# First-layer product in three two-part products, inputs split a chunk early, native products side by side, stores first on the load engine

## The chip, the core and the metric

One core of a Trainium2 chip runs the whole kernel. It has TensorE (PE, with its weight loads shown apart as PEld), VectorE (DVE), ScalarE (ACT), GpSimd (POOL, which issues the indexed gathers) and SyncE (SP, which issues the plain loads and stores). The metric is device time of one execution in microseconds (us): median of three runs, 5016.33 us before the change.

## The reference

Two graph layers run over 12500 nodes and 200000 edges, which are sorted by their target `dst`. What matters here is the first one:

```python
wk = relu(e @ k_w1 + k_b1) @ k_w2 + k_b2        # e: [E, 64], weights per edge
wv = relu(e @ v_w1 + v_b1) @ v_w2 + v_b2
k  = wk * sum_s sh[:, s] * (x[src] @ Cqk[:, s, :])   # s = 0..8, 64 -> 128
v  = wv * sum_s sh[:, s] * (x[src] @ Cv[:, s, :])
attn = einsum('ehd,ehd->eh', q[dst], k)         # softmax over the edges of a node
upd  = segment_sum(v * softmax(attn), dst)
x    = layernorm(x + batchnorm(x @ W_self + upd @ W_out))
```

The second layer takes the mean of the edges' features per node (a segment sum of `e`), and passes it with `x` through three small dense layers. Everything is float32. (In the code the roles of source and target in the index are those of the prepared inputs.)

## The kernel before

A first block prepares tables and weights. The main block, on which nearly all of the time is spent, goes over the edges in 392 chunks of 512. After it come a short block that mends segments over tile borders, and the node work.

**Two-part numbers.** A native float32 product on TensorE is slow, so the large products are made of parts: a float32 value is rounded to the type `float32r` (names that end in `hi`), the rest is what is left (`lo`), and a product is taken as hi*hi + lo*hi + hi*lo, three fast products. The tensor products (L825, L827, L828) and the second dense layer (L837 to L840) are done so. Native float32 are: the turns of the gathered rows and of the edge features (transposes, L797 and L813), the first dense layer (L807), and the segment sums (L855).

**One chunk, in short names.** PE: X turns the gathered rows `gx` (L797). H is the first dense layer into `hbank` (L807; `w1` against `e2`, a tile that holds two chunks, one in each half of the partitions). TP is 56 products (`tensor_products`). F turns the features of both chunks of a pair back into `hbank` (L813, only where `c.r` is odd). S0 and S1 are the halves of the segment sums (`sums`, L855): each has two products of a 0/1 matrix `seg` with the rows `rv`. EW is 16 products (`edge_weights`, L837 to L840). A and its sister turn scores and maxima, each once in four chunks (L879, L883). ACT copies out of PSUM (`ww` L572, `hid` L586, `rv` of F L595, `ot` L609), rounds to the high part (`zhi` L580, `hidhi` L601) and makes `seg` in `segments`: four ACTIVATE into `far` (L625), then one into `seg` (L630). DVE makes `z`, all of the low parts, the scores and the scans. POOL issues four gathers `gx` (L530) and four gathers `gq` (L535) for a chunk, and each fourth chunk one of another kind and a small copy.

**What sets the order.** Each engine has a function `step(t, ...)` written out by hand; `steps` calls it for every t (with a hardware loop of UN = 8 steps in the middle), and an engine runs its instructions in that order, each behind its semaphore waits. In step t the front works on chunk c = t+1, TP on chunk t, and the segment sums on b = t-6 (`LAG`). `segments(b+1)` on ACT makes the matrix that PE uses in the next step, in `sums(b, 0)` behind that step's TP. SP's order is loads of the harmonics `shb`, of the features, of the row `drow` for `segments`, of the masks `nmf` and `nmb` (the same numbers, one element apart), and then the store of the rows.

The few lines that the prediction's steps touch, on ACT and on PE:

```python
if c.r % 2 == 1:
    feature_rows(c + (-1))      # ACT, waits for F (et_full)
...
if (b + 1).there():
    segments(b + 1)             # ACT, sets seg_done
...
if half == 0:                   # PE, sums(b, 0)
    pe.wait_ge(pv_done, n)
    pe.wait_ge(seg_done, n)
```

Of the kernel before, what the change touches and what calls it, by code (L numbers as in the profile page):

```python
# [84 lines left out]
def steps(engine, step):  # L85
# [12 lines left out]
assert FINDS * TURNS + (NC + LAG + 1 - R0 - UN * TURNS) >= NT + 1 >= FINDS * TURNS  # L98


def gnn_kernel(nc, xg, xT, idx, dnow, dbefore, dlast, shT, eT, Wq, Ctp, W1, b1, Wk2, Wv2, b2, Wout, Wself, gamma_beta,
# [3 lines left out]
    newd = dram("newd", (EP + P,), bf16)  # L105
# [5 lines left out]
    with ctx:  # L111
# [7 lines left out]
        chi = sb("chi", [P, ST, KV], f32r)  # L119
        clo = sb("clo", [P, ST, KV], f32r)  # L120
        w1 = sb("w1", [P, 2, P])
        b1c = sb("b1c", [P, 1])
        w2hi = sb("w2hi", [P, KV], f32r)
        w2lo = sb("w2lo", [P, KV], f32r)
        b2hl = sb("b2hl", [P, KV], f32r)
        ones = sb("ones", [P, P], f32r)
# [12 lines left out]
        idx_all = sb("idx_all", [P, 2 * EC], i32)  # L139
        ndcol = sb("ndcol", [P, EC])  # L140
# [11 lines left out]

        load = sem("load")
# [3 lines left out]
        with ExitStack() as prep:  # L157
# [3 lines left out]
            ctp = ps("ctp", [P, ST, KV])  # L161
            w2 = ps("w2", [P, KV])
# [10 lines left out]
            npad = ps("npad", [2, P // 2], bf16)  # L173
# [24 lines left out]
            with nc.Block() as block:  # L198
                @block.sync
                def _(sp):  # L200
# [20 lines left out]
                    sp.wait_ge(neg_made, 3)  # L221
                    sp.dma_start(newd[0:EP].rearrange("(p c) -> p c", p=P), neg[:, :]).then_inc(tables_stored, 16)
                    sp.dma_start(newd[EP:EP + P].rearrange("(p c) -> p c", p=2), npad[:, :]).then_inc(tables_stored, 16)
# [6 lines left out]
                    sp.wait_ge(tables_stored, 64)  # L230
# [62 lines left out]
                def _(dve):  # L293
# [13 lines left out]
                    v.memset(npad[:, :], -BIG).then_inc(neg_made, 1)  # L307
# [11 lines left out]
                    dve.wait_ge(neg_made, 2)  # L319
# [16 lines left out]
                    dve.wait_ge(w_split, 6)  # L336
# [34 lines left out]
        with ExitStack() as main:  # L371
# [7 lines left out]
            nmf = ms("nmf", [P, 2, P], bf16)  # L379
            nmb = ms("nmb", [P, 2, P], bf16)  # L380
# [40 lines left out]
            et_full, et_done = sem("et_full"), sem("et_done")  # L421
            at_full, mf_done, mr_done, mt_full, mg_done, below_done = (
# [12 lines left out]
            with nc.Block() as block:  # L435
                @block.sync
                def _(sp):
# [27 lines left out]
                    def masks(g):  # L465
# [4 lines left out]
                        for ahead, tile in ((0, nmf), (1, nmb)):  # L470
# [86 lines left out]
                def _(act):  # L557
# [74 lines left out]
                    def step(t, find, fetch, count):  # L632
# [17 lines left out]
                        if b.there():  # L650
                            sums(b, 1)
# [804 lines left out]
```

## Time and profile before

| | |
|---|---|
| median of 3 runs | 5016.33 us (5014.75 to 5017.49) |
| the profiled execution | 5049.76 us, span 5047.8 us |
| mean granted TensorE clock | 0.975 |
| PE busy | 4772.7 us (95%) |
| DVE busy | 4058.6 us (80%) |
| POOL busy | 3713.3 us (74%), and 0.3 us before each gather that is not counted as busy |
| ACT busy | 3414.7 us (68%) |
| moved by DMA | 1006.45 MB, mean 199 GB/s |

A busy share is a mean over the whole span. The 0.975 comes from the end of the kernel: in the long main part the granted clock is 1.00. A matmul's record is longer than the time that it holds the engine, since matmuls are pipelined: what one costs is read from the distance between the starts of records. A native float32 matmul leaves two records.

### The profile page before, as it was taken

What the parts mean: (1) busy time and instruction counts of PE and PEld (TensorE: products, weight loads), DVE (VectorE), ACT (ScalarE), POOL (GpSimd) and SP (SyncE); (2) the same over time, 40 slices, a digit from 0 to 9 for tenths busy, and PEclk for the clock granted to TensorE, in tenths of its full rate; (3) what the DMA queues carried; (4) which work ended last, traced back from release to release, by engine and by line L of the source; (5) the groups of instructions that cost most, each with busy time, mean ns of one, the idle gap of its engine ahead of it and who ended that gap; (6) DMA issues with size and microseconds to landing.
All of it is one profiled execution on the core that took longest, in us unless ns stands there. A gap on an engine that the chain in (4) does not pass through costs nothing. (4 is left out here: it accounts for less than half of the span.)

```text
span 5047.8 us, 115383 instructions
## 1 busy us (share of the span) xinstructions
PE 4772.7 (95%) x35582; PEld 4503.5 (89%) x35582; DVE 4058.6 (80%) x5044; ACT 3414.7 (68%) x6495; POOL 3713.3 (74%) x3494
## 2 busy tenths in 40 slices
PE   7999999999999999999999999999999999998256
PEld 6999999999999999999999999999999999998143
DVE  5888888888888888888888888888888888886435
ACT  2677677677777767767777677777777777776137
POOL 3777777777777777777777777777777777774460
PEclk9999999999999999999999999999999999998578
DMA  8899999999999999999999999999999999996220
GB/s 218 202 215 210 208 210 214 208 214 210 212 207 214 213 208 213 211 210 211 211 213 211 207 216 213 216 214 214 213 216 212 214 214 216 212 213 158 91 68 26
DMA packets 693458, 1006.45 MB, mean 199 GB/s; under 512 B 120054, under 2 KB 378168, under 8 KB 693160
## 3 DMA queue, kind: packets, MB, share of 16 engines
q1 hardware_dynamic: 574856, 753.93, 65.7%
q0 software_dynamic: 112960, 242.16, 22.7%
q10 hardware_dynamic: 5600, 9.83, 0.7%
q8 instruction: 22, 0.36, 0.0%
q14 instruction: 20, 0.16, 0.0%
HBM read 826.64 MB, written 178.93 MB: 199 GB/s over the span
## 5 line engine op out<-in xcount | busy, mean ns | idle before, releaser
L825 PE MATMUL psum<-chi,zhi 128*128 128x256 f32 x7840 | 2316.9, 301 | 2.2 <-DVE rv L731 2.1
L535 POOL DMA_INDIRECT gq<-qtab,idxs x1568 | 1881.1, 1200 | 478.0 <-issue 475.8
L828 PE MATMUL psum<-clo,zhi 128*128 128x256 f32 x7840 | 2144.4, 282 | 0.0
L530 POOL DMA_INDIRECT gx<-in_xg,idxs x1568 | 1555.4, 992 | 465.0 <-issue 453.5
L827 PE MATMUL psum<-chi,zlo 128*128 128x256 f32 x6272 | 1768.4, 282 | 0.0
L825 PEld LDWEIGHTS psum<-chi,zhi 128*128 128x128 f32 x7840 | 1478.6, 189 | 99.3 <-issue 99.3
L828 PEld LDWEIGHTS psum<-clo,zhi 128*128 128x128 f32 x7840 | 1476.2, 188 | 0.0
L827 PEld LDWEIGHTS psum<-chi,zlo 128*128 128x128 f32 x6272 | 1183.6, 189 | 93.0 <-issue 93.0
L685 DVE TENSOR_TENSOR z<-psum,shb 128x1536 f32<-128x1536 f32 (+1 forms) x784 | 1130.5, 1483 | 126.2 <-PE psum L797 118.7
L580 ACT ACTIVATE zhi<-z 128x1536 fp32r<-128x1536 f32 (+1 forms) x784 | 993.5, 1267 | 247.9 <-DVE z L685 244.0
L710 DVE TENSOR_TENSOR zlo<-z,zhi 128x1536 fp32r<-128x1536 f32 (+1 forms) x784 | 922.2, 1217 | 0.0
L609 ACT ACTIVATE ot<-psum 128x400 f32<-128x400 f32 x784 | 389.0, 496 | 518.0 <-PE psum L855 513.2
L706 DVE TENSOR_TENSOR hidlo<-hid,hidhi 128x512 fp32r<-128x512 f32 x392 | 271.5, 693 | 536.3 <-ACT hidhi L601 526.2
L855 PE MATMUL psum<-rv,seg 128*128 128x200 f32 x3136 | 669.9, 337 | 20.8 <-DVE rv L693 16.7
L855 PEld LDWEIGHTS psum<-rv,seg 128*128 128x128 f32 x3136 | 512.3, 192 | 27.3 <-DVE rv L693 19.6
L625 ACT ACTIVATE far<-drow,ndcol 128x128 f32<-128x128 bf16 x1568 | 501.5, 390 | 13.1 <-issue 0.5
L837 PE MATMUL psum<-b2hl,ones 128*128 128x256 f32 x1568 | 496.8, 317 | 4.8 <-DVE hidlo L706 4.8
L840 PE MATMUL psum<-w2lo,hidhi 128*128 128x256 f32 x1568 | 442.4, 282 | 0.0
L839 PE MATMUL psum<-w2hi,hidlo 128*128 128x256 f32 x1568 | 441.8, 282 | 0.0
L838 PE MATMUL psum<-w2hi,hidhi 128*128 128x256 f32 x1568 | 441.4, 282 | 0.0
L595 ACT ACTIVATE rv<-psum 128x512 f32<-128x512 f32 x196 | 117.3, 598 | 465.1 <-PE psum L813 465.1
L572 ACT ACTIVATE ww<-psum 128x1024 f32<-128x1024 f32 x392 | 397.1, 1013 | 15.7 <-PE psum L840 15.6
(210 smaller groups left out, 6335.1 us busy)
## 6 DMA issues: line engine op xcount, KB each, us to landing
shb<-in_shT SPq DMA_DIRECT2D x392, 640.0 KB
shb<-in_shT SPq DMA_DIRECT2D x392, 512.0 KB
rows<-ot SPq DMA_DIRECT2D x392, 416.0 KB
e<-in_eT SPq DMA_DIRECT2D x392, 128.0 KB
drow<-rankd SPq DMA_DIRECT2D x392, 128.0 KB
gx<-in_xg,idxs POOLq DMA_INDIRECT x1568
gq<-qtab,idxs POOLq DMA_INDIRECT x1568
qtab<-qs ACTq DMA_DIRECT2D x25, 256.0 KB, 5.7
```

Of the source, the lines that this page charges most:

```text
L530: nc.gpsimd.indirect_dma_start(out=gx[:, s, k, :], out_offset=None, in_=xg[:, :], in_offset=bass.IndirectOffsetOnAxis(ap=ids[:, k:k + 1], ...
L535: nc.gpsimd.indirect_dma_start(out=gq[:, s, k, :], out_offset=None, in_=qtab[:, :], in_offset=bass.IndirectOffsetOnAxis(ap=ids[:, TC + k:T ...
L580: f(zhi[:, s, j, :], z[:, j, :], ACT.Copy).then_inc(zhi_done, 1)
L625: f(far[:, k * P:(k + 1) * P], drow[:, s, k * P:(k + 1) * P], ACT.Abs, bias=ndcol[:, bass.ds(b.value() * TC + k, 1)]).then_inc(far_done, 1)
L685: v.tensor_tensor(z[:, j, :], xbank.unsqueeze(1).broadcast_to([P, n, CH]), shb[:, s, j, :], ALU.mult).then_inc(z_done, 1)
L710: rest = lambda j: v.tensor_tensor(zlo[:, s, j, :], z[:, j, :], zhi[:, s, j, :].bitcast(fp32), ALU.subtract).then_inc(zlo_done, 1)
L825: mm(tpb[:, k, :], zhi[:, s, j, e], chi[:, j, :], start=(j == 0), stop=False)
L827: mm(tpb[:, k, :], zlo[:, s, j, e], chi[:, j, :], start=False, stop=False)
L828: last = mm(tpb[:, k, :], zhi[:, s, j, e], clo[:, j, :], start=False, stop=(j == ST - 1))
L837: mm(wb[:, k, :], ones[:, :], b2hl[:, :], start=True, stop=False)
L840: last = mm(wb[:, k, :], hidhi[:, e], w2lo[:, :], start=False, stop=True)
L855: last = mm(gbank[:, 256 * k:256 * k + O + D + H], seg[:, s, t * P:(t + 1) * P], rv[:, b.slot(UN), t, :], start=True, stop=True)
```

## The change

It does these things:

1. The first dense layer is taken in three two-part products. `w1` is split once, in the first block, into `w1hi` and `w1lo`. The features of a pair of chunks are split as well: ACT makes `e2hi` (`features_first_part`) and DVE `e2lo` (`features_rest`), once for two chunks, in the step before the pair's first product.
2. The segment sums are of chunk a = t-7 rather than b = t-6, and they stand on PE around X and H: S0, X, H, S1, TP, F, EW. The natives thus lie side by side (but for H, which is native no more). `seg_done` is waited for as before.
3. ACT's step has a new order. It starts with the copy of S0, takes `hidden` before `zhi`, `hidhi` before the second part of `zhi`, and ends with `segments(b)`, which stands behind `feature_rows`.
4. SP's step starts with the store (of chunk t-8), and loads `drow` for t-5 rather than t-4.
5. The masks are loaded once into `nmf`, one element wider, and the backward scan reads it shifted.
6. Some SBUF is freed earlier (`edges.close()`), and in the last block several semaphores become one for each engine.

```diff
@@ steps @@
-    for n in range(R0 + UN * TURNS, NC + LAG + 2):
+    for n in range(R0 + UN * TURNS, NC + LAG + 3):
...
@@ first block, DVE @@
+                    v.tensor_copy(w1hi[:, :, :], w1[:, :, :]).then_inc(w_split, 1)
...
+                    v.tensor_tensor(w1lo[:, :, :], w1[:, :, :], w1hi[:, :, :].bitcast(fp32), ALU.subtract)
...
@@ main block, SP @@
-                            sp.wait_ge(h_full, c.value() - 2)
+                            sp.wait_ge(e2lo_done, c.turn(2) - 1)
...
-                        for ahead, tile in ((0, nmf), (1, nmb)):
-                            src = newd[bass.ds(g.value() * CH + ahead, GT * P)].rearrange("(t e) -> t e", t=GT)
-                            sp.dma_start(tile[:, s, :], src.unsqueeze(1).broadcast_to([GT, H, P])).then_inc(nm_in[s], 16)
+                        src = newd[bass.ds(g.value() * CH, GT * P)].rearrange("(t e) -> t e", t=GT)
+                        sp.dma_start(nmf[:, s, 0:P], src.unsqueeze(1).broadcast_to([GT, H, P])).then_inc(nm_in[s], 16)
...
                     def step(t, find, fetch, count):
+                        if (t + (-LAG - 2)).there():
+                            store(t + (-LAG - 2))
                         if (t + 2).there():
                             harmonics(t + 2)
                         if (t.r + 3) % 2 == 0 and (t + 3).there():
                             features(t + 3)
-                        if (t + (2 - LAG)).there():
-                            targets(t + (2 - LAG))
+                        if (t + (1 - LAG)).there():
+                            targets(t + (1 - LAG))
...
-                        if (t + (-LAG - 1)).there():
-                            store(t + (-LAG - 1))
@@ main block, ACT @@
+                    def features_first_part(c):
+
+                        act.wait_ge(e_in[c.r // 2 % 2], 32 * (c.turn(4) + 1))
+                        if c.old(2):
+                            act.wait_ge(h_full, c.value())
+                        f(e2hi[:, :], e2[:, c.r // 2 % 2, :], ACT.Copy).then_inc(e2hi_done, 1)
...
-                        c, b = t + 1, t + (-LAG)
+                        c, b, a = t + 1, t + (-LAG), t + (-LAG - 1)
+                        if a.there():
+                            sums(a, 0)
+                        if t.there():
+                            edge_weights(t)
                         if b.there():
                             weights(b)
-                        if t.there():
-                            edge_weights(t)
+                        if c.there():
+                            hidden(c)
+                        if a.there():
+                            sums(a, 1)
+                            maxima(a)
+                        if (c + 1).there() and c.r % 2 == 1:
+                            features_first_part(c + 1)
                         if c.there():
                             z_first_part(c, 0)
-                            hidden(c)
+                            hidden_first_part(c)
                             z_first_part(c, 1)
-                            hidden_first_part(c)
                             if c.r % 2 == 1:
                                 feature_rows(c + (-1))
                         if b.there():
-                            sums(b, 0)
-                            maxima(b)
-                        if (b + 1).there():
-                            segments(b + 1)
-                        if b.there():
-                            sums(b, 1)
+                            segments(b)
@@ main block, DVE @@
+                    def features_rest(c):
+                        dve.wait_ge(e2hi_done, c.turn(2) + 1)
+                        if c.old(2):
+                            dve.wait_ge(h_full, c.value())
+                        v.tensor_tensor(e2lo[:, :], e2[:, c.r // 2 % 2, :], e2hi[:, :].bitcast(fp32), ALU.subtract).then_inc(e2lo_done, 1)
...
                             hidden_rest(c)
+                        if (c + 1).there() and c.r % 2 == 1:
+                            features_rest(c + 1)
+                        if c.there():
                             z_rest(c)
@@ main block, PE @@
                     def hidden(c):
-                        s = c.r // 2 % 2
-                        pe.wait_ge(e_in[s], 32 * (c.turn(4) + 1))
+                        pe.wait_ge(e2lo_done, c.turn(2) + 1)
...
-                        mm(hbank, w1[:, c.r % 2, :], e2[:, s, :], start=True, stop=True).then_inc(h_full, 1)
+                        k = c.r % 2
+                        mm(hbank, w1hi[:, k, :], e2hi[:, :], start=True, stop=False)
+                        mm(hbank, w1hi[:, k, :], e2lo[:, :], start=False, stop=False)
+                        mm(hbank, w1lo[:, k, :], e2hi[:, :], start=False, stop=True).then_inc(h_full, 1)
...
                     def step(t, find, fetch, count):
-                        c, b = t + 1, t + (-LAG)
+                        c, a = t + 1, t + (-LAG - 1)
+                        if a.there():
+                            sums(a, 0)
                         if c.there():
                             turned_x(c)
                             hidden(c)
+                        if a.there():
+                            sums(a, 1)
                         if t.there():
                             tensor_products(t)
                         if c.there() and c.r % 2 == 1:
                             turned_features(c + (-1))
-                        if b.there():
-                            sums(b, 0)
                         if c.there():
                             edge_weights(c)
-                        if b.there():
-                            sums(b, 1)
```

The line numbers shift: L595 (`rv` of F) becomes L611, L609 (`ot`) L625, L615 L631, L625 (`far`) L641, L630 (`seg`) L646, L661 (`signs`) L680, L572 (`ww`) L581; on PE L797 becomes L829, L813 L847, L837 to L840 L871 to L874, L855 L889, L879 L913.

On ACT, in a step with F, this is what stands behind the turned features before the change (from the first ACTIVATE that waits for F to the copy of the second half of the sums):

```order
329 L591 REGISTER_ALU
330 L593 REGISTER_ALU [waits et_full]
331 L595 ACTIVATE rv<-psum 128x8x64 [waits sum_full]
332 L605 REGISTER_ALU
333 L609 ACTIVATE ot<-psum 128x2x200 [waits rows_stored0,sum_full]
334 L615 ACTIVATE ot<-mg 128x4x8 [waits ota_done]
335 L625 ISA [waits drow_in1,seg_done]
...
344 L629 ISA [waits far_done]
345 L630 ACTIVATE seg<-far 128x512 [waits sum_full]
346 L605 REGISTER_ALU
347 L609 ACTIVATE ot<-psum 128x2x200 [waits sum_full]
```

And after it, from the second part of `zhi` to the copy that begins the next step:

```order
338 L589 ACTIVATE zhi<-z 128x1024 [waits tp_full,z_done]
339 L607 REGISTER_ALU
340 L609 REGISTER_ALU [waits et_full]
341 L611 ACTIVATE rv<-psum 128x8x64 [waits sum_full]
342 L636 ISA
343 L641 ISA [waits drow_in0,seg_done]
...
352 L645 ISA [waits far_done]
353 L646 ACTIVATE seg<-far 128x512 [waits sum_full]
354 L621 REGISTER_ALU
355 L625 ACTIVATE ot<-psum 128x2x200 [waits rows_stored0,sum_full]
356 L581 ACTIVATE ww<-psum 128x1024 [waits vv_done,w_full]
```

The copies of the sums have moved away from between; the `seg` made here is now the one of the sums at the head of PE's next step.

On PE, before the change, from the end of a TP with F to the second dense layer:

```order
1064 L828 MATMUL psum<-clo,zhi 128x256
1065 L811 REGISTER_ALU
1066 L813 MATMUL psum<-idn,e 128x128 [waits hid_done]
1067 L813 MATMUL psum<-idn,e 128x128 x3
1068 L846 REGISTER_ALU
1069 L848 REGISTER_ALU [waits seg_done,pv_done]
1070 L855 MATMUL psum<-rv,seg 128x200 [waits otb_done,et_done]
1071 L855 MATMUL psum<-rv,seg 128x200
1072 L837 MATMUL psum<-b2hl,ones 128x256 [waits ww_done,hidlo_done]
```

And after it, from the last product of the second dense layer over the border to the next step:

```order
1112 L874 MATMUL psum<-w2lo,hidhi 128x256
1113 L912 REGISTER_ALU [waits attn_done]
1114 L913 MATMUL psum<-idn,attn 128x128 [waits mg_done]
1115 L880 REGISTER_ALU
1116 L882 REGISTER_ALU [waits seg_done,pv_done]
1117 L889 MATMUL psum<-rv,seg 128x200 [waits otb_done,et_done]
1118 L889 MATMUL psum<-rv,seg 128x200
1119 L827 REGISTER_ALU [waits x_gathered2]
1120 L829 MATMUL psum<-idn,gx 128x128 [waits z_done]
1121 L829 MATMUL psum<-idn,gx 128x128 x3
...
1123 L839 MATMUL psum<-e2hi,w1hi 128x512 [waits et_done,hid_done,e2lo_done]
```

S0 stood behind TP and F, with X and H ahead; now it stands behind EW (and A), and X, H, S1 and TP are queued behind it.

## Rows read from the trace of the kernel before

**Rows 1.** Busy time by stretch: engines' busy us (instructions), granted clock, DMA share, GB/s.
```profile
400.00:2400.00 2000.00, 1978.51 (x15133) 1886.84 (x15132) 1691.59 (x2054) 1416.55 (x2692) 1576.05 (x1454) 1.00 0.95 211
3000.00:4600.00 1600.00, 1600.00 (x12279) 1529.58 (x12278) 1371.15 (x1665) 1148.27 (x2189) 1251.50 (x1181) 1.00 0.96 214
```

**Rows 2.** Who waited for whom, whole span: us in total, times, longest.
```profile
DVE hidlo L706 <- ACT hidhi L601: 526.2, 384, 2.5
ACT rv L595 <- PE psum L813: 465.1, 196, 2.9
PE psum L797 <- DMA gx<-in_xg,idxs: 43.5, 22, 16.0
```

**Rows 3.** PE's timeline, a chunk with F and A: start, us, line, xcount.
```profile
2513.89 0.60 PE L797 MATMUL psum<-idn,gx 128*128 128x128 f32 x4
2514.33 1.02 PE L807 MATMUL psum<-e,w 128*128 128x512 f32 x2
2514.79 0.68 PE L825 MATMUL psum<-chi,zhi 128*128 128x256 f32 x1
2515.31 0.28 PE L827 MATMUL psum<-chi,zlo 128*128 128x256 f32 x1
...
2521.78 0.28 PE L828 MATMUL psum<-clo,zhi 128*128 128x256 f32 x1
2521.90 0.60 PE L813 MATMUL psum<-idn,e 128*128 128x128 f32 x4
2522.34 0.84 PE L855 MATMUL psum<-rv,seg 128*128 128x200 f32 x4
...
2523.13 0.28 PE L838 MATMUL psum<-w2hi,hidhi 128*128 128x256 f32 x1
...
2524.92 0.84 PE L855 MATMUL psum<-rv,seg 128*128 128x200 f32 x4
2525.60 0.27 PE L879 MATMUL psum<-idn,attn 128*128 128x128 f32 x1
2525.70 0.60 PE L797 MATMUL psum<-idn,gx 128*128 128x128 f32 x4
```

**Rows 4.** ACT's timeline, the same chunk.
```profile
2519.64 0.63 ACT L601 ACTIVATE hidhi<-hid 128x512 fp32r<-128x512 f32 x1
2522.61 0.60 ACT L595 ACTIVATE rv<-psum 128x512 f32<-128x512 f32 x1 [2.35 <-PE psum L813]
2523.21 0.51 ACT L609 ACTIVATE ot<-psum 128x400 f32<-128x400 f32 x1
...
2523.95 1.28 ACT L625 ACTIVATE far<-drow,ndcol 128x128 f32<-128x128 bf16 x4
2525.36 0.63 ACT L630 ACTIVATE seg<-far 128x512 f32<-128x512 f32 x1
```

**Rows 5.** DVE's timeline, the same chunk.
```profile
2520.30 0.69 DVE L706 TENSOR_TENSOR hidlo<-hid,hidhi 128x512 fp32r<-128x512 f32 x1 [1.53 <-ACT hidhi L601]
2520.91 2.36 DVE L710 TENSOR_TENSOR zlo<-z,zhi 128x1536 fp32r<-128x1536 f32 x2
```

**Rows 6.** POOL's timeline, the same chunk.
```profile
2519.95 0.94 POOL L535 DMA_INDIRECT gq<-qtab,idxs  x1 [0.30 <-issue]
2521.19 2.29 POOL L535 DMA_INDIRECT gq<-qtab,idxs  x1 [0.30 <-issue]
```

**Rows 7.** All instructions that touch the tile gx: ns min/median/max, first and last start.
```profile
L797 PE MATMUL psum<-idn,gx x1568: 271/273/476, 78.1 to 4620.5; 128*128 128x128 f32 x196
```

**Rows 8.** PE's timeline at one of its waits for a gather.
```profile
958.20 0.84 PE L855 MATMUL psum<-rv,seg 128*128 128x200 f32 x4
961.32 0.65 PE L797 MATMUL psum<-idn,gx 128*128 128x128 f32 x4 [2.28 <-DMA gx<-in_xg,idxs]
```

**Rows 9.** Timeline of PE and PEld at 4631: a weight load, and its matmul.
```profile
4631.11 0.65 PEld L855 LDWEIGHTS psum<-rv,seg 128*128 128x128 f32 x4
4631.23 0.84 PE L855 MATMUL psum<-rv,seg 128*128 128x200 f32 x4
```

More of the change, by code:

```diff
@@ L151, in gnn_kernel, with eb @@
         banks = [psum[:, i * 512:(i + 1) * 512] for i in range(8)]
+        edges = ctx.enter_context(ExitStack())
+        def eb(name, shape, dt=fp32):
+            return edges.enter_context(nc.sbuf_tensor(name, shape, dt))
+        chi = eb("chi", [P, ST, KV], f32r)
+        clo = eb("clo", [P, ST, KV], f32r)
+        w1hi = eb("w1hi", [P, 2, P], f32r)
+        w1lo = eb("w1lo", [P, 2, P], f32r)
+        b1c = eb("b1c", [P, 1])
+        w2hi = eb("w2hi", [P, KV], f32r)
+        w2lo = eb("w2lo", [P, KV], f32r)
+        b2hl = eb("b2hl", [P, KV], f32r)
+        ones = eb("ones", [P, P], f32r)
+        idx_all = eb("idx_all", [P, 2 * EC], i32)
+        ndcol = eb("ndcol", [P, EC])
         load = sem("load")
@@ L161, in gnn_kernel @@
             ctp = ps("ctp", [P, ST, KV])
+            w1 = ps("w1", [P, 2, P])
             w2 = ps("w2", [P, KV])
@@ L378, in gnn_kernel @@
             drow = ms("drow", [P, 2, CH], bf16)
-            nmf = ms("nmf", [P, 2, P], bf16)
-            nmb = ms("nmb", [P, 2, P], bf16)
+            nmf = ms("nmf", [P, 2, P + 1], bf16)
+            e2hi = ms("e2hi", [P, CH], f32r)
+            e2lo = ms("e2lo", [P, CH], f32r)
             hid = ms("hid", [P, CH])
@@ L744, in segment_maxima @@
                         dve.wait_ge(at_full, n)
[L745 removed]
+                        dve.wait_ge(nm_in[s], 16 * (g.turn(2 * GC) + 1))
                         if g.old(GC):
                             dve.wait_ge(mt_full, n - 1)
[L748 removed]
+                        v.tensor_tensor_scan(mf[:, :], nmf[:, s, 0:P], sbank[:, 0:P], -BIG, ALU.add, ALU.max).then_inc(mf_done, 1)
                         dve.wait_ge(mf_done, n)
[L750 removed]
+                        v.tensor_tensor_scan(mr[:, ::-1], nmf[:, s, P:0:-1], mf[:, ::-1], -BIG, ALU.add, ALU.max).then_inc(mr_done, 1)
                     def below_maxima(g):
@@ L885, in _ @@
                     steps(pe, step)
+        edges.close()
         with ExitStack() as mend:
@@ L1085, in gnn_kernel @@
             st_d, st_a, st_pe = sem("stats_dve"), sem("stats_act"), sem("stats_pe")
-            SS = {k: sem(f"{k}_made") for k in ("r", "y", "dd", "sq", "lg", "rs", "x1", "s0", "h0", "h1", "y2", "dd2", "sq2",
-                                                "lg2", "rs2", "o")}
-            prod_made = sem("products_made")
-            PRODUCTS = ("mean", "var", "z0", "z1", "z2", "mean2", "var2")
+            MADE = {"pe": ("mean", "var", "z0", "z1", "z2", "mean2", "var2"),
+                    "act": ("r", "sq", "lg", "rs", "h0", "h1", "sq2", "lg2", "rs2"),
+                    "dve": ("y", "dd", "x1", "s0", "y2", "dd2", "o")}
+            made_by = {e: sem(f"blocks_made_by_{e}") for e in MADE}
             def wait_made(engine, name, i, j):
-                if name in PRODUCTS:
-                    engine.wait_ge(prod_made, (i * len(PRODUCTS) + PRODUCTS.index(name)) * GN + (j + 1))
-                else:
-                    engine.wait_ge(SS[name], i * GN + (j + 1))
+                for e, names in MADE.items():
+                    if name in names:
+                        engine.wait_ge(made_by[e], (i * len(names) + names.index(name)) * GN + (j + 1))
             with ExitStack() as fin1:
@@ L1293, in product @@
                                 wait_made(pe, after, i, j)
-                                t.matmul(bank_of(j), lhsT[:, :], W(src, j), start=True, stop=True).then_inc(prod_made, 1)
+                                t.matmul(bank_of(j), lhsT[:, :], W(src, j), start=True, stop=True).then_inc(made_by["pe"], 1)
                         def turn(i):
```

50 lines of the change are left out of this document (19 added, 31 removed).

## The prediction

> **What bounds the kernel now.** I read the busy times by stretch first, then the waits, then the timelines of PE, ACT, DVE and POOL over one chunk, and last the view of one tile, for the whole main loop. By stretch, PE is busy for all of 3000 to 4600 us and for 1978.51 of 2000 us before that, at a granted clock of 1.00 [rows 1]. So the order of PE's instructions and what each costs there sets the time; other engines count only where PE waits for them. The waits show one such place of weight: before X, for gathered rows, 43.5 us in 22 waits, of which one of 16.0 us is the start; 21 are left with 27.5 us [rows 2].
>
> What each piece costs is read from the distances of PE's starts [rows 3]. X: 2513.89 to 2514.33, 0.44 us. TP: from its second product at 2515.31 to its last at 2521.78 there are 54 steps, 0.1198 each, so 56 take 6.71. H is what is left of 2514.33 to 2521.90: 7.57 - 6.71 = 0.86. F: 0.44. S0 and EW: 2522.34 to 2524.92, 2.58; the 16 products of EW at nearly the step of TP's are 1.91, S0 is 0.67. S1: 0.68. A: 0.10. The sum is 11.81, which is the distance from X to X: nothing is idle. A chunk without F and A is 11.27. A pair of chunks has one F and on average one A or its sister: 2 x 11.27 + 0.44 + 0.10 = 23.08, 11.54 per chunk. Over the whole loop, the last chunk's X is at 4620.5 (less 0.3, as that is its fourth turn) and the first at 78.1 [rows 7]: 4542 us over 391 chunks, 11.617. The 0.08 above 11.54 is 31 us in all, which is the waits for gathers.
>
> **The change, part by part.**
>
> *H in three products.* 0.86 goes. No row shows a float32r product of 512 columns. The nearest is that of 256 columns at 0.1198. Twice that is 0.24, the upper end; 512 columns at 2.4 GHz, the level that a granted clock of 1.00 is, are 0.213, the lower end. I take 0.1198 plus 256 columns more at 2.4 GHz, 0.226. Three are 0.68 (0.64 to 0.72), the saving 0.18 per chunk (0.14 to 0.22), and over 392 chunks -71 us (-55 to -86).
> The Trainium skill (TensorE: Matmul & The Clock Gate, section "Wait — 56ns, not 53.3ns?") gives N / 2.4 GHz plus 2.5 ns from start to start. By that, as an estimate, three would take 0.65 and the saving be 83 us. At 256 columns it gives 0.109 where the rows have 0.1198, so the trace does not agree, and I stay with the rows.
>
> *Splitting the features.* ACT's `e2hi` and DVE's `e2lo` have the size of `hidhi` and `hidlo`, 0.63 and 0.69, once for a pair [rows 4, 5]. ACT's lies in the same step in which it waits 2.35 us for F; DVE waits 1.53 us for `hidhi` in each chunk, in total 526.2 us [rows 2, 5], and `hidhi` now comes earlier. Nothing for both. Without that cover `e2lo` would cost 0.69 per pair, 135 us.
>
> *The place of S0 and S1.* Moving them costs PE no time by itself: in rows 3 the change from float32r to native and back (TP to F to S0 to EW) shows no gap. What changes is when S0 comes, and what it waits for. It waits for `seg_done`. Before, `seg` was made on ACT in step t and used behind TP in step t+1, some 8 us later. Now `segments(b)` is the last thing in ACT's step t and S0 of the same chunk is the first in PE's step t+1. In a step with F, ACT stands in `feature_rows`, which waits for F (2.35 us in rows 4; 465.1 us in 196 waits, rows 2), and `segments` is queued behind it. So from the start of F on PE, called 0:
> - ACT starts `rv` (L595) at 0.71 (2521.90 to 2522.61) and its next ACTIVATE 0.60 later, at 1.31; now that is `far`.
> - From the start of `far` at 2523.95 to the end of `seg`, 2525.36 + 0.63 = 2525.99, are 2.04: `seg` is ready at 3.35 [rows 4].
> - A finished ACT operation lets the next engine start 0.03 later (`hidhi` ends at 2520.27, `hidlo` starts at 2520.30, rows 4 and 5); then `seg` is loaded as weights, 0.12 before the matmul [rows 9]. S0 can start at 3.50.
> - PE has F and EW to do until then: 0.44 + 1.91 = 2.35, with A 2.45.
> PE then stands idle for 1.15, with A 1.05: 1.10 on average in each pair, and with it all that is queued behind S0: X, H, S1, TP. It can't be caught up, since the next F comes only after that TP. Of the 196 steps with F the first three have no sums yet: 193 x 1.10 = +212 us. Without the handover of the weight load, or with a slower start of `far` behind its wait for `drow` (0.15), it is 1.00 to 1.25, +193 to +241 us.
> In a step without F nothing is late: ACT is through `hidhi` at 2520.27 in rows 4, 2.04 more would be 2522.3, and S0 would want it after 2524.9. S1 waits for the copy of S0 (0.51, rows 4), but X and the new H, 1.12, lie between them. TP's other partner, DVE, has the same sequence as before with a shorter wait in it.
>
> *SP's order, masks, semaphores.* The loads keep their places in the cycle; only the store comes a little sooner. `nmb` was 32 KB per four chunks of some 10 MB (1006 MB over 98 times four chunks). Nothing on the path. The drain has one step more, with what ACT does in it (two copies of 0.51, `far` and `seg` 2.04): +3 us; the first split, +1 us.
>
> *The waits for gathers.* POOL issues without a pause: in 400 to 2400 us 1576.05 busy and 1454 instructions with the 0.30 us of issue before each (436) fill the 2000 [rows 1, 6]. It gets more time: a pair takes 23.08 - 0.36 + 1.10 = 23.82, 0.74 longer. I expect the waits to go, up to -31 us.
>
> **The sum**, against the profiled execution: 5049.76 - 71 + 212 + 4 = 5195, less 31 = 5164 us; per chunk 11.91. The median before lies 33 us below the profiled execution, about what the waits for gathers cost there. If runs without a profile have none of them, the median goes to 5016.33 + 145 = 5161; if they have them and lose them, to 5130. I take 5150.
> PE's new idle times should not lower its clock: idle of 2.28 us at one place [rows 8] stands in a stretch of mean clock 1.00 [rows 1].
>
> **The rivals.**
> *R1, `seg` is in time and PE gets faster (other side).* The place is S0 in the steps with F. It holds if ACT's chain from F's start to the end of `seg` is under 2.3 us rather than 3.35; each 0.1 less gives 19 us, and it decides at a wait of 0.37 per pair, where the saving in H is eaten up. For it: ACT is idle 32% of the span, so it has room. Against it: `far` and `seg` alone take 2.04 in every chunk, and they can't start before `feature_rows` in program order. It gives 5016.33 - 71 + 4 = 4949, if POOL follows; it is full already at 11.54 per chunk, so up to 5016.
> *R2, POOL becomes a second bound.* The gather at 2521.19 took 2.29 us and the one before it 0.94; the long one lies under DVE's `zlo` [rows 5, 6], a subtraction with both inputs in SBUF. `e2lo` is one more of this kind, 0.69 per pair. If all of it lands on POOL it takes 0.69 of the 0.74 that POOL gains, and waits for gathers stay or double beside the wait for `seg`: 5161 + 34 = 5195.
> The Trainium skill (GPSIMD Engine Reference, section "Key points") says that GpSimd shares its SBUF interfaces with VectorE and contends with instructions with two SBUF inputs; rows 5 and 6 fit it, and by it alone the change would cost up to 135 us of POOL's time.
> *R3, the two terms cancel* or the reordering does nothing measurable: a wait of 0.3 to 0.45 us per pair, 5006 to 5026.
>
> **How the numbers follow.** Forecast 0.78, R1 0.07, R2 0.12, R3 0.03. A measurement of this kernel tells about 0.2% (10 us) from no change. Faster by more than that: R1, 0.07. Within: 0.03. Slower: forecast and R2, 0.90. The likeliest case's own range is 5016.33 - 86 + 193 + 4 - 31 = 5096 to 5016.33 - 55 + 241 + 4 = 5206. With R1 left out and R2 inside, the range is 5098 to 5202, the time 5150.
>
> **What would show it.** In the waits: a new row in which PE's segment sums wait for ACT's `seg`, some 193 times, 1.0 to 1.2 us each, 210 us in all. In PE's timeline: idle of that length between EW (or A) and S0 in every other chunk and none in the others; from X to X 12.7 us (3.50 from F's start to S0 in place of 2.4) and 11.1 in turn, mean 11.91; starts of the first layer's products 0.22 to 0.24 apart. In ACT's: `far` directly behind the copy of F. DVE's waits for `hidhi` shorter, and no or few waits for gathers. It is wrong if PE is busy throughout again, if the idle stands before X or TP, or if each of the three products takes much more than 0.24.

## The result, and the profile after

The changed kernel takes 5445.38 us (median of 4 runs, 5430.95 to 5447.62), the kernel before 5016.91 us (4 runs, 5014.75 to 5021.02): a ratio of 1.0847 [1.0827, 1.0867] (the brackets hold its 95% interval, here and below). That is slower by 428 us; the forecast was 5150, slower by 134. The direction was right, and two thirds of the loss were not in it. The profiled run took 5445.56 us.

The page's line of busy times, and from its table of queues the one that carries instructions:

```profile
PE 4818.5 (89%) x35974; PEld 4638.8 (85%) x35974; DVE 4186.2 (77%) x5242; ACT 3389.0 (62%) x6691; POOL 3822.1 (70%) x3494
...
q14 instruction: 251, 2.06, 0.1%
```

PE was busy for 95% of the span before and is now for 89%. Queue q14 had 20 packets with 0.16 MB before; it has 251 with 2.06 MB now. At 0.1% of the DMA engines' time it looks like nothing.

Busy time by stretch, the answer to [rows 1]: length, busy us (instructions) of PE, PEld, DVE, ACT, POOL, granted clock, DMA share, GB/s.

```profile
400.00:2400.00 2000.00, 1839.28 (x14075) 1791.35 (x14074) 1605.35 (x1966) 1292.38 (x2557) 1482.60 (x1339) 0.97 0.86 194
3000.00:4600.00 1600.00, 1473.53 (x11286) 1435.05 (x11285) 1286.76 (x1575) 1035.47 (x2051) 1188.59 (x1074) 0.97 0.86 194
```

Where PE was busy for all of 1600 us it is now idle for 126, and the clock, 1.00 before, is 0.97. Who waited for whom, from 300 to 5000 us (total, times, longest), in place of [rows 2]:

```profile
ACT ot L625 <- issue: 246.7, 46, 6.3
PEld psum L889 <- issue: 215.2, 185, 1.3
...
PE psum L889 <- ACT ot L625: 190.7, 46, 5.1
DVE hidlo L726 <- ACT hidhi L617: 174.9, 232, 2.0
PE psum L889 <- ACT seg L646: 144.6, 138, 1.1
...
PE psum L889 <- issue: 34.2, 47, 0.8
```

The waits for gathers are gone, and there are two new causes. One is the forecast's: S0 waits for `seg`, 138 + 47 times (where `seg` was seen last, and where nothing was), and its weight loads stand idle 185 times for 1.16 us each. The other was not forecast: ACT, 46 times, waits for nothing that the profile shows ("issue"), 5.4 us each, and S1 on PE waits behind it 46 times, 4.1 us each. 46 is the number of turns of the main loop in that window, one per eight chunks.

PE's timeline over one chunk without a turn, in place of [rows 3]:

```profile
2507.12 0.60 PE L829 MATMUL psum<-idn,gx 128*128 128x128 f32 x4
2507.48 0.48 PE L839 MATMUL psum<-e2hi,w1hi 128*128 128x512 f32 x1
2507.80 0.40 PE L840 MATMUL psum<-e2lo,w1hi 128*128 128x512 f32 x1
2508.03 0.39 PE L841 MATMUL psum<-e2hi,w1lo 128*128 128x512 f32 x1
2508.26 0.84 PE L889 MATMUL psum<-rv,seg 128*128 128x200 f32 x4
2508.80 0.42 PE L859 MATMUL psum<-chi,zhi 128*128 128x256 f32 x1
2509.06 0.28 PE L861 MATMUL psum<-chi,zlo 128*128 128x256 f32 x1
...
2515.54 0.60 PE L847 MATMUL psum<-idn,e 128*128 128x128 f32 x4
2515.89 0.36 PE L871 MATMUL psum<-b2hl,ones 128*128 128x256 f32 x1
...
2517.87 0.27 PE L913 MATMUL psum<-idn,attn 128*128 128x128 f32 x1
2518.87 0.92 PE L889 MATMUL psum<-rv,seg 128*128 128x200 f32 x4 [0.73 <-issue]
```

X and H together are 2507.12 to 2508.26, 1.14 us (1.30 before); from F to S0 are 3.33 us. Away from the turns, X to X is 12.74 with F (12.50 in one pair of four) and 11.0 to 11.1 without, 11.85 per chunk. Without the wait for `seg` it is 11.25 (`a_both_zsplit` below), so the wait costs 1.21 per pair.

Now ACT's timeline at a turn of the loop (start, duration, instruction, and in brackets the idle time before it and what ended it):

```profile
2440.51 0.63 ACT L646 ACTIVATE seg<-far 128x512 f32<-128x512 f32 x1
2441.05 0.65 ACT L674 ACTIVATE signs<-grow,nodeh 128x448 bf16<-128x448 int32 x1
2441.61 0.19 ACT L674 ACTIVATION_READ_ACCUMULATOR signs<-grow,nodeh  x1
2446.63 0.50 ACT L625 ACTIVATE ot<-psum 128x400 f32<-128x400 f32 x1 [4.84 <-issue]
```

Of the queues, this is q14 in the pause alone, 2441.8 to 2446.6 us (packets, MB, share):

```profile
q14 instruction: 2, 0.02, 1.4%
```

PE's timeline at the same turn:

```profile
2442.25 0.60 PE L829 MATMUL psum<-idn,gx 128*128 128x128 f32 x4
...
2443.16 0.40 PE L841 MATMUL psum<-e2hi,w1lo 128*128 128x512 f32 x1
2447.19 1.70 PE L889 MATMUL psum<-rv,seg 128*128 128x200 f32 x4 [3.64 <-ACT ot L625]
...
2449.33 0.41 PE L859 MATMUL psum<-chi,zhi 128*128 128x256 f32 x1
2449.54 0.41 PE L861 MATMUL psum<-chi,zlo 128*128 128x256 f32 x1
...
2459.54 0.60 PE L829 MATMUL psum<-idn,gx 128*128 128x128 f32 x4
```

`ot`, the first instruction of ACT's loop body, starts 4.84 us after ACT is done with the last. The waits show nothing that holds it: S0's result has been there since 2442.2. Two instruction packets are moved in the pause, and 5 in the 100 us from 2400 to 2500, in which there is this one turn. S1 then starts at 2447.19 in place of 2443.39 (0.23 behind the last of H): 3.80 us. X to X is 17.29 where 11.0 is usual, 6.3 more, so some 2.5 are lost after the idle. The granted clock has them, by busy time of short stretches of the same turn (columns as above):

```profile
2429.80:2442.20 12.40, 11.33 (x90) 11.00 (x89) 10.22 (x12) 8.94 (x18) 9.96 (x9) 1.00 0.89 201
...
2447.20:2450.20 3.00, 3.00 (x12) 3.00 (x13) 1.29 (x2) 2.82 (x6) 1.32 (x3) 0.50 0.15 48
2450.20:2453.20 3.00, 3.00 (x19) 3.00 (x19) 1.73 (x2) 3.00 (x7) 2.23 (x2) 0.63 0.68 188
2453.20:2459.50 6.30, 6.30 (x54) 6.30 (x53) 3.80 (x6) 1.85 (x6) 5.00 (x5) 1.00 1.06 221
```

Behind the idle 3.64 us PE runs at 0.50, the level of 1.2 GHz: S1 takes twice its time, and products come 0.21 apart in place of 0.12. The idle 0.7 to 1.1 for `seg`, in the first stretch, leave it at 1.00. Over all turns the eight chunks take 101.5 us, without the turn's excess they would take 94.8: 6.7 x 46 = 308 us. The miss is 295.

### The profile page after: what moved, and what is told of

It reads as the page before. It is cut to its first block and busy times, and to the rows that moved or that the text cites. A ratio compares the mean times of both kernels' runs of the same rounds, so it can differ in the third digit from the quotient of the medians.

```text
span 5443.7 us, 116993 instructions
## 1 busy us (share of the span) xinstructions
PE 4818.5 (89%) x35974; PEld 4638.8 (85%) x35974; DVE 4186.2 (77%) x5242; ACT 3389.0 (62%) x6691; POOL 3822.1 (70%) x3494
## 3 DMA queue, kind: packets, MB, share of 16 engines
q14 instruction: 251, 2.06, 0.1%
## 5 line engine op out<-in xcount | busy, mean ns | idle before, releaser
L859 PE MATMUL psum<-chi,zhi 128*128 128x256 f32 x7840 | 2238.2, 292 | 0.0
L539 POOL DMA_INDIRECT gx<-in_xg,idxs x1568 | 1761.9, 1124 | 673.8 <-issue 460.0
L544 POOL DMA_INDIRECT gq<-qtab,idxs x1568 | 1750.3, 1116 | 477.9 <-issue 477.2
L859 PEld LDWEIGHTS psum<-chi,zhi 128*128 128x128 f32 x7840 | 1513.3, 193 | 0.3
L862 PEld LDWEIGHTS psum<-clo,zhi 128*128 128x128 f32 x7840 | 1507.5, 192 | 0.0
L861 PEld LDWEIGHTS psum<-chi,zlo 128*128 128x128 f32 x6272 | 1212.1, 193 | 0.3
L625 ACT ACTIVATE ot<-psum 128x400 f32<-128x400 f32 x784 | 399.4, 509 | 1104.7 <-PE psum L889 856.7
L889 PE MATMUL psum<-rv,seg 128*128 128x200 f32 x3136 | 723.8, 356 | 396.5 <-ACT ot L625 196.2
L589 ACT ACTIVATE zhi<-z 128x1536 fp32r<-128x1536 f32 (+1 forms) x784 | 1008.4, 1286 | 1.2 <-DVE z L705 1.2
L889 PEld LDWEIGHTS psum<-rv,seg 128*128 128x128 f32 x3136 | 556.9, 199 | 491.1 <-issue 240.7
L641 ACT ACTIVATE far<-drow,ndcol 128x128 f32<-128x128 bf16 x1568 | 498.6, 397 | 0.0
L611 ACT ACTIVATE rv<-psum 128x512 f32<-128x512 f32 x196 | 117.4, 599 | 576.5 <-PE psum L847 576.5
L871 PE MATMUL psum<-b2hl,ones 128*128 128x256 f32 x1568 | 455.6, 291 | 3.4 <-DVE hidlo L726 3.4
L874 PE MATMUL psum<-w2lo,hidhi 128*128 128x256 f32 x1568 | 439.2, 280 | 0.0
L581 ACT ACTIVATE ww<-psum 128x1024 f32<-128x1024 f32 x392 | 399.8, 1020 | 22.3 <-PE psum L874 22.3
```

The source lines that it names most:

```text
L539: nc.gpsimd.indirect_dma_start(out=gx[:, s, k, :], out_offset=None, in_=xg[:, :], in_offset=bass.IndirectOffsetOnAxis(ap=ids[:, k:k + 1], ...
L544: nc.gpsimd.indirect_dma_start(out=gq[:, s, k, :], out_offset=None, in_=qtab[:, :], in_offset=bass.IndirectOffsetOnAxis(ap=ids[:, TC + k:T ...
L589: f(zhi[:, s, j, :], z[:, j, :], ACT.Copy).then_inc(zhi_done, 1)
L641: f(far[:, k * P:(k + 1) * P], drow[:, s, k * P:(k + 1) * P], ACT.Abs, bias=ndcol[:, bass.ds(b.value() * TC + k, 1)]).then_inc(far_done, 1)
L859: mm(tpb[:, k, :], zhi[:, s, j, e], chi[:, j, :], start=(j == 0), stop=False)
L861: mm(tpb[:, k, :], zlo[:, s, j, e], chi[:, j, :], start=False, stop=False)
```

## The experiments

Theory T: at the end of ACT's loop body the first instructions of the next turn are no longer at hand and must be loaded again, through q14. The change made ACT's loop longer (309 instructions in the built program, 297 before) and let it begin elsewhere (after 270, not 268), so that it ends after 579, not 565. Rivals: it is the new order on ACT (R), or the loop's length alone (T1), or its position (T3). The other half of the plan was the forecast's own term: undo the wait for `seg` and see what is left. Times of the kernel before are given per batch, since batches ran on different chips.

**First batch** (before: 5025.47 us, 13 runs). Before's kernel with idle instructions in ACT's loop, and nothing else:

```diff
 def step(t, find, fetch, count):        # ACT
     c, b = t + 1, t + (-LAG)
+    for _ in range(1 + t.r % 2):
+        act.sem_inc(act_passed, 1)
```

> The kernel before with 12 idle semaphore increments more in ACT's loop body of eight steps (12 instructions more, as many as the change adds there), nothing else. Theory T1 (ACT's loop body has become too long for what the engine keeps of its program, so that it is loaded again by DMA at each turn): the queue q14 of instruction transfers goes from 20 packets to about 250, ACT shows a wait of 4 to 6 us on issue at each of the 47 turns, and PE is late by 2 to 5 us at each: 5110 to 5250 us. Rival T2 (the wait at the turns comes of the new order of ACT's step, which begins with the copy of S0): no change, 5010 to 5025 us, 20 packets.

5216.87 us, ratio 1.0362 [1.0286, 1.0438]; q14 has 251 packets. The idle instructions also stand in the steps written out ahead of the loop, which so ends after 593 instructions. Waits from 300 to 4500 us:

```profile
ACT rv L565 <- issue: 219.5, 44, 6.1
...
PE psum L839 <- DVE hidlo L708: 126.5, 44, 3.3
```

So the pause comes with no change in the work at all, and the new order is not its cause.

The changed kernel with `e2hi` made on DVE, which takes ACT's loop down to 299 instructions. The steps ahead of it are shorter too, so that it ends after 556: length and place change together.

```diff
-    if (c + 1).there() and c.r % 2 == 1:          # ACT
-        features_first_part(c + 1)
...
 def features_rest(c):                             # DVE
+    v.tensor_copy(e2hi[:, :], e2[:, c.r // 2 % 2, :]).then_inc(e2hi_done, 1)
```

> The changed kernel with e2hi made by DVE instead of ACT: ACT's loop body is as long as before the change again (10 instructions less), and its order is that of the change. T1: q14 back at about 20 packets, no wait on issue at the turns, the distance X to X at the turn back from 17.6 to 11.0 us, 46 times 6.6 us less: 5130 to 5150 us. T2: within 20 us of 5445. The wait for seg stays: 0.9 us in each pair.

5139.36 us, 1.0213 [1.0138, 1.0287]; 21 packets; 94.86 us per eight chunks, all of them. PE still waits for `seg`. With the pause gone, what is left is near the forecast.

The changed kernel with ACT's `segments` ahead of `feature_rows`:

```diff
+    if b.there():
+        segments(b)
-            if c.r % 2 == 1:
-                feature_rows(c + (-1))
-    if b.there():
-        segments(b)
+    if c.there() and c.r % 2 == 1:
+        feature_rows(c + (-1))
```

> The changed kernel with segments(b) ahead of feature_rows in ACT's step. Theory S (seg queued behind the wait for F makes S0 late): the wait of PE for seg is gone, 0.9 to 1.0 us in each of 193 pairs: 175 to 195 us less than 5445, 5250 to 5270. ACT's loop body has the same length, so under T1 the waits at the turns stay. Rival: something else (DVE, S1's wait for the copy of S0) holds S0 as late, then within 40 us of 5445.

5230.86 us, 1.0402 [1.0325, 1.0479]: 214.5 us less than the changed kernel. The forecast's term was 212; expected here, from the idle times of PE alone, were 175 to 195. The wait for `seg` is gone, the 251 packets and the pause at the turn are not. The pause is longer than in the changed kernel, 6.5 us each in place of 5.4, so the 214.5 hold less than the whole wait: 193 pairs of 1.21 are 234.

Both edits together:

```diff
+        segments(b)                               # ACT, ahead of feature_rows(c + (-1))
...
-        features_first_part(c + 1)                # ACT
+    v.tensor_copy(e2hi[:, :], e2[:, c.r // 2 % 2, :]).then_inc(e2hi_done, 1)      # DVE
```

> Both edits: e2hi on DVE and segments(b) ahead of feature_rows. If T1 and S are right and independent, 5445 less 305 and less 185: 4940 to 4975 us, faster than the kernel before by 1% or so, which would be the three two-part products alone (0.16 to 0.18 us in each chunk). If POOL, which already issues without a pause, holds the rate: 5000 to 5040.

5061.0 us (10 runs), 1.006 [1.0032, 1.0088]: a miss, above both expected ranges. Undisturbed, eight chunks take 90.0 us; but their mean is 11.655 per chunk, since a third cause appears. First its waits, 300 to 4500 us, then POOL's timeline, then DVE's:

```profile
PEld psum L828 <- issue: 112.8, 72, 3.9
...
PE psum L828 <- DMA gx<-in_xg,idxs: 90.9, 54, 3.6
```

```profile
2458.85 0.94 POOL L544 DMA_INDIRECT gq<-qtab,idxs  x1 [0.31 <-issue]
2460.10 2.42 POOL L544 DMA_INDIRECT gq<-qtab,idxs  x1 [0.30 <-issue]
```

```profile
2459.34 0.69 DVE L731 TENSOR_TENSOR e2lo<-e,e2hi 128x512 fp32r<-128x512 f32 x1
2459.95 2.35 DVE L735 TENSOR_TENSOR zlo<-z,zhi 128x1536 fp32r<-128x1536 f32 x2
```

POOL does nothing but gathers, 0.30 apart, and doesn't keep up at 11.25 us per chunk. The gather that starts 0.15 into the `zlo` of 1536 columns takes 2.42 us, as in [rows 5, 6]. That led to the next question: is it the length of that one DVE instruction?

**Second batch** (before: 5020.61 us, 13 runs). Before's kernel, with 12 idle instructions ahead of ACT's loop and none in it:

```diff
+    for _ in range(12):
+        act.sem_inc(act_passed, 1)
     steps(act, step)
```

> The kernel before with 12 idle semaphore increments ahead of ACT's loop, none in it. T1 (the length of the loop body counts): no reload, q14 at about 20 packets, 5015 to 5035 us. Rival T3 (where the loop stands in the program counts, its start and end in blocks of what is loaded): a reload at each turn as with 12 in the body, q14 at about 250 packets, 5150 to 5250 us.

5170.21 us (a single run, no interval), 250 packets. The loop is as long as before's, so T1 (length alone) falls. ACT's waits (300 to 4300), and its timeline at a turn:

```profile
ACT rv L565 <- issue: 184.0, 42, 4.9
```

```profile
2410.71 0.19 ACT L655 ACTIVATION_READ_ACCUMULATOR signs<-grow,nodeh  x1
2415.21 0.23 ACT L565 ACTIVATE rv<-below 128x32 f32<-128x32 f32 x1 [4.31 <-issue]
```

Before's kernel with four in the loop (3 instructions more, as built):

```diff
+    if t.r % 2:
+        act.sem_inc(act_passed, 1)
```

> The kernel before with 4 idle semaphore increments more in ACT's loop body (3 instructions more as built, where 11 more reload and 2 more, with e2hi on DVE, do not). It narrows the length at which T1 sets in: either 20 packets and 5015 to 5035 us, or 250 packets and 5150 to 5250 us; I expect the former.

5188.31 us (a single run), 251 packets. A miss: I had expected no pause at 300 instructions. The loop ends after 573 here, after 565 in before's kernel and after 576 in the one above.

Before's kernel, its `zlo` of 1536 columns in three instructions of 512:

```diff
-    rest(slice(0, 3))
+    for j in range(2):
+        v.tensor_tensor(zlo[:, s, j, :], z[:, j, :], zhi[:, s, j, :].bitcast(fp32), ALU.subtract)
+    rest(slice(2, 3))
```

> The kernel before with DVE's zlo of 1536 columns (1.75 us, both inputs in SBUF) taken in three pieces of 512. Theory P (a gather on POOL that meets such an instruction waits for the end of that one instruction, so a short one holds it less): the gathers of 2.0 to 2.3 us are gone, none over 1.7; POOL gains some 0.5 us per chunk and waits for PE in places; no waits of PE for gathers, 11.53 per chunk: 5005 to 5020 us, at most 30 us faster, since PE is the bound. Rival (the gather waits for the whole chain of DVE's instructions): gathers as long as before, 5016 to 5030.

5009.92 us (10 runs), 0.9973 [0.995, 0.9996]. No wait for a gather is left on PE. From the page, the gathers of `gq` (busy us, mean ns, idle before them); they took 1881.1 us before, 1200 ns each:

```profile
L535 POOL DMA_INDIRECT gq<-qtab,idxs x1568 | 1517.7, 968 | 478.0 <-issue 475.5
```

Those of `gx` take 1037 ns, 992 before, so that a pair of gathers is shorter by 0.19 us. The gain over the kernel before is 0.3% or 11 us in this batch. That it comes of the split is not shown: `b_shift60`, below, has `zlo` whole and no wait for a gather on PE either, and takes as long. What the split does show is room: from 300 to 4500 us POOL's gathers of `gx` wait for DVE 169 times, 211 us in all; in the kernel before POOL has no such wait from 300 to 4300 us.

The changed kernel with all three edits:

```diff
+        segments(b)                               # ACT, ahead of feature_rows(c + (-1))
...
-        features_first_part(c + 1)                # ACT
+    v.tensor_copy(e2hi[:, :], e2[:, c.r // 2 % 2, :]).then_inc(e2hi_done, 1)      # DVE
...
-    rest(slice(0, 3))
+    for j in range(2):
+        v.tensor_tensor(zlo[:, s, j, :], z[:, j, :], zhi[:, s, j, :].bitcast(fp32), ALU.subtract)
+    rest(slice(2, 3))
```

> The changed kernel with e2hi on DVE, segments ahead of feature_rows, and zlo in three pieces. a_both took 5061 us though its undisturbed eight chunks took 90.0 us (11.25 each) against 92.2 before; its PE waited for gathers. Theory P: with the gathers' stalls shortened POOL keeps up, 11.25 to 11.3 per chunk: 392 times 0.35 to 0.4 us less than a_both, 4905 to 4940 us. Rival (PE's waits for gathers come of the DMA queues' load or of the landing time, not of POOL's pace): 5030 to 5065 us as a_both.

4896.15 us, 0.9739 [0.9681, 0.9797]: faster than both kernels, and 9 us below the range expected. 90.01 us per eight chunks, 11.25 each, and gathers of `gq` at 1006 ns where `a_both` had 1205. So what `a_both` lacked was the time of POOL under that instruction. Against `b_zsplit`, which has the same `zlo`, the change in this form is worth 114 us, more than the 71 that the forecast gave H.

**Third batch** (before: 5025.13 us, 7 runs). T3 had two forms: the loop may not cross some fixed place (T3b), or it is kept while it touches three blocks of the program and not while it touches four (T3a). By T3a a larger shift takes the pause away again. Before's kernel with 60 in place of 12:

```diff
+    for _ in range(60):
+        act.sem_inc(act_passed, 1)
     steps(act, step)
```

> The kernel before with 60 idle increments ahead of ACT's loop, where 12 made the reload appear. T3a (ACT's program is loaded in blocks of 8 KB, 128 instructions as the transfers of q14 suggest, and a loop of some 300 instructions is kept if it touches three blocks and loaded again at each turn if it touches four): 60 push its start over into the next block, it touches three again, and the reload is gone: about 20 packets, 5015 to 5035 us. Rival T3b (a fixed place in the program beyond which a loop is reloaded): about 250 packets and 5150 to 5200 us.

5010.44 us (a single run), 21 packets: more idle instructions, and no pause. T3b falls. The gathers of `gq` still take 1181 ns, and no PE wait for a gather is left. So the changed kernel needs no change in its work, only a shift:

```diff
+    for _ in range(50):
+        act.sem_inc(act_passed, 1)
     features_first_part(Chunk(0, 0))
     steps(act, step)
```

> The changed kernel with 50 idle increments ahead of ACT's loop and nothing else, so that its 309 instructions lie in three blocks. T3a: about 20 packets on q14, no wait on issue at the turns, 5135 to 5150 us, which is what the forecast's terms give without the reload. T3b: 5440 us.

5141.43 us, 1.0219 [1.0149, 1.029]. From its page, and its waits (300 to 4700 us):

```profile
q14 instruction: 22, 0.18, 0.0%
```

```profile
PE psum L891 <- ACT seg L646: 144.4, 138, 1.1
```

This splits the loss: 5445.38 - 5141.43 = 304 us are the pause at the turn, and the 116 that stay against before's kernel of this batch are what the forecast described (together 420, not 428: the batches ran on different chips, and their times of the kernel before differ by 8).

The best order with `e2hi` left on ACT:

```diff
+        segments(b)                               # ACT, ahead of feature_rows(c + (-1))
...
+    for _ in range(50):                           # ACT, ahead of the loop
+        act.sem_inc(act_passed, 1)
...
-    rest(slice(0, 3))                             # DVE
+    for j in range(2):
+        v.tensor_tensor(zlo[:, s, j, :], z[:, j, :], zhi[:, s, j, :].bitcast(fp32), ALU.subtract)
+    rest(slice(2, 3))
```

> The changed kernel with its splitting of the features left on ACT, segments(b) ahead of feature_rows, zlo in three pieces, and the 50 idle increments: 11.25 us per chunk, 4895 to 4905 us, like a_both_zsplit (4896). Under T3b with the reload, 5150 to 5200 us.

4896.75 us, 0.9733 [0.9667, 0.9799]: the same as with `e2hi` on DVE, so which engine makes `e2hi` counts only by what it does to ACT's program.

Last, what does the change's order give apart from H? H in three products and `zlo` in three, the split of the features on DVE, and before's order on PE, ACT and SP (the diff is against the changed kernel, its part on ACT):

```diff
-    c, b, a = t + 1, t + (-LAG), t + (-LAG - 1)
-    if a.there():
-        sums(a, 0)
...
-    hidden_first_part(c)
+    hidden(c)
     z_first_part(c, 1)
+    hidden_first_part(c)
...
-    segments(b)
+    sums(b, 0)
+    maxima(b)
...
+    segments(b + 1)
...
+    sums(b, 1)
```

> The order before the change on PE, ACT and SP, with the first layer in three products, the features split on DVE, and zlo in three pieces. If the place of S0 and S1 is worth nothing on PE: 11.53 less 0.18 = 11.35 per chunk, 4935 to 4945 us. If natives side by side save the 0.10 us by which a_both_zsplit's 11.25 lies below that, it stays at 11.35; if the three products are worth all of the 0.28, it is 11.25 and 4896 us.

5144.45 us, 1.0224 [1.0154, 1.0293], with 21 packets: a miss by 200 us. Its waits (300 to 4500 us), and DVE's timeline over a step:

```profile
ACT zhi L589 <- DVE z L701: 493.1, 354, 3.1
DVE hidlo L722 <- ACT hidhi L617: 450.3, 354, 1.3
...
PE psum L859 <- DVE rv L757: 160.1, 275, 1.2
```

```profile
2510.20 2.88 DVE L701 TENSOR_TENSOR z<-psum,shb 128x1536 f32<-128x1536 f32 x2
...
2515.54 0.69 DVE L722 TENSOR_TENSOR hidlo<-hid,hidhi 128x512 fp32r<-128x512 f32 x1 [1.27 <-ACT hidhi L617]
2516.15 0.42 DVE L728 CAST e2hi<-e 128x512 fp32r<-128x512 f32 x1
2516.61 0.69 DVE L730 TENSOR_TENSOR e2lo<-e,e2hi 128x512 fp32r<-128x512 f32 x1
...
2521.70 0.68 DVE L764 TENSOR_REDUCE attn<-kq 128x32 f32<-128x512 f32 x1
```

DVE does `z`, ACT makes `zhi`, `hid`, the second `zhi` and then `hidhi`, DVE waits 1.27 us for that, and goes on to the next `z` at 2522.3: a closed round of 12.1 us in the step with the features, in which PE has no part and waits in its TP. This is read from the rows; no run takes it apart. In the changed order `hidhi` comes ahead of the second `zhi`, and DVE's waits for it fall to 174.9 us. By this reading, the reordering is worth no time on PE but room for the split.

## Why the prediction was right in sign and wrong in size

**The step that failed** is "ACT's `e2hi` ... Nothing for both". No run shows a cost of its engine time. But the change's new instructions on ACT, and where its loop begins, brought a cost that has no instruction: 304 us by `a_shift50`, 46 pauses of 5.4 us on ACT that make 6.7 each on PE. The sum had priced every instruction, and had no term for bringing the instructions themselves to ACT. [Rows 4] could not warn, since before's loop happens to be kept; `b_shift12` shows how near it was to 5170 us.

**H in three products.** Forecast 0.68, so 0.18 less per chunk. Measured, X and H together fall from 1.30 to 1.14: 0.16, inside its 0.14 to 0.22. The products start 0.32, 0.23, 0.23 apart; the forecast's step was 0.226. The first takes 0.09 more, and X ahead of them 0.08 less (0.36 for 0.44).

**S0's wait for `seg`.** The named row came, 185 times (193 forecast, over all of the loop). Forecast 3.50 from F to S0, measured 3.33. Per pair 1.10 was forecast; the weight loads' idle is 1.16, and by the distances from X to X the wait costs 1.21, 234 us for the forecast's 212. X to X was to be 12.7 and 11.1 in turn and is 12.74 and 11.0 to 11.1; the mean away from the turns is 11.85, forecast 11.91; without the pause the time is 5141, forecast 5150.

**What made up for the small differences.** That 5141 lies so near 5150 is in part luck: the wait is some 22 us dearer than forecast and H gives 8 less, and TP is cheaper. Without any wait a chunk takes 11.25, not the 11.36 of the forecast's terms. The step within TP is 0.1178 (2509.06 to 2515.42 in the changed kernel, 54 steps), in [rows 3] it is 0.1198: 0.11 per chunk, 43 us in all. That wasn't foreseen, and its cause stays open; it comes with H in three products (last section).

**Waits for gathers** went, as forecast (up to -31 us). R2 didn't come true in the changed kernel: PE has no wait for a gather, nor has it in `a_shift50`, where POOL still issues without a pause. But its mechanism is real: when PE could go at 11.25, POOL is the bound (`a_both`, +165 us against `a_both_zsplit`). The Trainium skill (GPSIMD Engine Reference, section "Key points") says that GpSimd contends with DVE instructions with two SBUF inputs; these runs agree, and add that the length of the one DVE instruction counts, not their total: `b_zsplit` has the same columns in three pieces, and its `gq` gathers take 968 ns, not 1200 (`gx` 1037, not 992).

**PE's clock.** "PE's new idle times should not lower its clock" held for those that were forecast, 0.7 to 1.1 us, and not for those that weren't. Its ground was weak: the trace of the kernel before has, beside the 2.28 us of [rows 8], a wait for a gather of 2.55 us with a clock of 0.50 behind it (last section), which the mean of [rows 1] hides.

**R1** needed `seg` in time. It isn't in this kernel; with `segments` first and the pause and POOL's bound out of the way, the time is 4896, below R1's 4949 mainly by the 0.11 in TP (43 us) and by before's waits for gathers, which `b_zsplit` and `b_shift60` lack (some 11 to 15). **R3** had the two terms cancel; they don't.

## What to carry to other kernels

Compare the instruction queue's packets and the engines' "issue" waits at the turns of a loop before and after every edit, also of an edit that costs no engine time: a pause there is no matter of the work but of the program's length and place, and a few idle instructions can bring it or take it away. Where an instruction feeds the next step's first consumer, put it ahead of whatever waits for another engine in the same step. When one wait goes, work out at what rate each other engine can follow: here POOL did 11.65 us a chunk in `a_both`, and shorter DVE instructions let it follow at 11.25.

## What the hardware showed unexpectedly

- **ACT's program is loaded again at a loop's turn, by place.** Where the loop ends after 556, 565, 624 and 628 instructions q14 has 21 or 22 packets, after 573, 576, 579 and 593 it has 250 or 251: 230 more in 46 turns, 5 per turn, 8 KB each, and a pause of 4.4 (`b_shift12`) to 6.5 us (`a_seg_first`) on average. Loops of 297 instructions are in both groups. Blocks of 128 instructions, of which three are kept and four are not, fit all eight if the first block is put to suit; so do blocks of 256, of which two are kept and three are not. No run shows the blocks themselves, nor why 5 packets come. The price was 150 us in `b_shift12`, 168 in `b_pad4`, 191 in `b_pad12`, 304 here. On PE no such pause shows: in `a_shift50` X to X over the turn is 11.0, as usual.
- **The length of an idle time alone doesn't tell PE's clock behind it.** After 3.64 us idle in the turn shown the granted clock is 0.50 for the next 3 us, and it is at most 0.57 behind each of the 42 turns between 150 and 4500 us (3.31 us idle and more). This makes 3.8 us of lateness 6.3. But after 2.28 us [rows 8] it is 1.00, after 2.55 us in the same kernel it is 0.50, and after 3.24 us in `b_pad12` it is 1.00. Busy times by stretch, `before` and then `b_pad12`, clock third from the end:

```profile
2831.30:2834.30 3.00, 3.00 (x8) 1.97 (x9) 1.56 (x1) 0.33 (x1) 2.09 (x4) 0.50 1.07 274
1865.10:1868.10 3.00, 2.98 (x23) 2.95 (x24) 2.94 (x4) 1.02 (x4) 2.54 (x2) 1.00 0.23 53
```

- **A gather's time goes by the length of one DVE instruction.** It is 2.42 us under a `zlo` of 1536 columns (`a_both`), and none is over 1.5 where that is in pieces of 512 (`b_zsplit`, `a_both_zsplit`). That it waits for the end of the instruction fits this, and no run takes it further.
- **The step of a 256-column product isn't fixed.** Within TP it is 0.1198 in nearly every chunk of the kernels with the native H (`before`, `b_zsplit`, `b_shift60`), and 0.1178 in those with H in three products, also in `b_h3_zsplit` with the order of before; there about a quarter of the chunks have 0.1133. So it goes with H and not with the order. Why is not explained.
